# Logits in eight 64x32 tiles, one spread per piece, a ring of five pieces, and token sums at other places of the PE queue

## The reference, cut to what matters

```python
# block 1, per image
y = ln_c(x)                                   # norm over channels, per pixel
g = groupnorm(y, 8 groups) * gn_w + gn_b
x = x + y + w2 @ relu(w1 @ g + b1) + b2
# block 2, per image, tokens = pixels
t = tokens(x); z = ln(t)                      # norm over the 64 channels of a token
logits = z @ gate_w.T + gate_b                # 32 experts
vals, idx = top_k(softmax(logits, over pixels), 8)       # 8 pixels per expert
pooled = sum_k vals[k] * z[idx[k]]            # 64 numbers per expert
out = gelu([pooled, 1] @ weight1) ; out = [out, 1] @ weight2
t[idx[k]] += out * vals[k]                    # the rest of t is unchanged
```

## Time and profile before

| | us |
|---|---|
| median of 3 runs | 639.11 (637.3 to 641.03) |
| the profiled execution | 639.6 |
| its span, first to last instruction | 637.9 |
| PE / DVE / ACT / POOL busy | 535.4 / 487.2 / 435.3 / 189.6 |
| x1 (L948), 64 instructions | 82.1 |
| logits (L409), 1024 matmul records | 69.4 |
| sums (L372) of x, of centred squares, of x1's squares | 74.5 + 35.7 + 34.1 |
| mean granted TensorE clock | 0.935 |

### The profile page before, as it was taken

The page is one execution under the profiler, slowest core; times in us unless marked ns, Lnnn a source line. Parts: engine busy times, 40 slices in busy tenths (PEclk is TensorE's granted clock), DMA queues, the critical chain, the costliest instruction groups (busy, mean ns, idle before and its releaser), DMA issues.

```text
span 637.9 us, 14170 instructions
## 1 busy us (share of the span) xinstructions
PE 535.4 (84%) x5732; PEld 270.3 (42%) x5732; DVE 487.2 (76%) x950; ACT 435.3 (68%) x651; POOL 189.6 (30%) x116
## 2 busy tenths in 40 slices
PE   2749999898998899889989899989887988876982
PEld 1324444444444344444444444444443433434762
DVE  5574556689888988898789878988888687799620
ACT  2463779677976797679767976797677855984110
POOL 1007435023502260217020802080207145121144
PEclk9955999999999999999999999999998998987595
DMA  8960144714471447244634454445401255430000
GB/s 195 195 144 0 68 133 142 188 68 133 133 199 67 134 133 191 76 133 134 168 98 134 115 160 123 133 101 165 133 35 67 76 182 154 146 100 5 6 15 19
DMA packets 26752, 73.38 MB, mean 115 GB/s; under 512 B 4152, under 2 KB 4152, under 8 KB 22592
## 3 DMA queue, kind: packets, MB, share of 16 engines
q1 hardware_dynamic: 25664, 71.44, 40.9%
q0 software_dynamic: 1024, 1.05, 0.6%
HBM read 38.40 MB, written 34.08 MB: 114 GB/s over the span
## 4 chain that ended last, share of the span: by engine, by line
PE 41%; DVE 30%; ACT 13%; issue 12%; DMA 2%; POOL 1%; SPq 0%; ACTq 0%; DVEq 0%; POOLq 0%
PE st L372 11%; ACT junk L801 7%; DVE xs L948 7%; PE cv L383 6%; PE cv L391 6%; PE tl L400 6%; PE bc L494 5%; DVE us L938 5%; DVE lg L936 3%; DVE top_i L1035 2%; ACT tok L766 2%; DVE us L940 2%; DVE cnd L1030 2%; DMA xs<-in_x 2%; PE tl L409 2%
## 5 line engine op out<-in xcount | busy, mean ns | idle before, releaser
L1426 POOL TENSOR_TENSOR xs<-xs,us 128x1024 f32<-128x1024 f32 x64 | 151.2, 2379 | 367.2 <-DVE xs L948 173.4
L948 DVE SCALAR_TENSOR_TENSOR xs<-cv,vecs,xs 128x1024 f32<-128x1024 f32 x64 | 82.1, 1282 | 47.8 <-PE cv L391 47.7
L794 ACT ACTIVATE sqc<-us 128x1024 f32<-128x1024 f32 x64 | 67.5, 1054 | 46.2 <-DVE us L938 45.4
L761 ACT ACTIVATE hid<-cv,b1n 128x1024 f32<-128x1024 f32 x64 | 71.2, 1113 | 36.5 <-PE cv L383 36.0
L938 DVE TENSOR_TENSOR us<-xs,bc 128x1024 f32<-128x1024 f32 x60 | 73.0, 1216 | 19.7 <-PE bc L494 19.3
L400 PEld LDWEIGHTS tl<-ident,xs 128*128 128x128 f32 x512 | 63.8, 195 | 53.9 <-issue 53.9
L372 PE MATMUL st<-xs,stat_w 128*32 128x256 f32 x1024 | 74.5, 413 | 10.5 <-DMA xs<-in_x 9.4
L801 ACT ACTIVATE junk<-us 128x1024 bf16<-128x1024 f32 x64 | 67.3, 1051 | 22.8 <-DVE gsum L940 22.1
L940 DVE CUSTOM_DVE_ANT_0 us<-us,bc 128x1024 f32<-128x1024 f32 x60 | 72.9, 1215 | 11.2 <-PE bc L494 9.9
L400 PE MATMUL tl<-ident,xs 128*128 128x128 f32 x512 | 76.4, 294 | 0.9 <-ACT lg L776 0.9
L409 PE MATMUL tl<-xs,gcen 128*32 128x256 f32 x1024 | 69.4, 389 | 8.0 <-ACT tok L766 7.9
(11 more groups left out here) (210 smaller groups left out, 652.4 us busy)
## 6 DMA issues: line engine op xcount, KB each, us to landing
xs<-in_x SPq DMA_DIRECT2D x64, 512.0 KB, 7.0
out_rows<-tok SPq DMA_DIRECT2D x64, 512.0 KB
us<-in_e_w SPq DMA_DIRECT2D x8, 260.0 KB
xs<-in_e_w SPq DMA_DIRECT2D x8, 256.0 KB
sqc<-out_rows,idx_all POOLq DMA_INDIRECT x16
out_rows<-sqc,idx_all POOLq DMA_INDIRECT x16, 2.1
vecs<-in_b SPq DMA_DIRECT2D x4, 0.2 KB, 14.0
gate_bias<-in_gate_b SPq DMA_DIRECT2D x4, 0.1 KB, 12.3
```

The source lines that it names most:

```text
L948: nc.vector.scalar_tensor_tensor(out=xu, in0=cv[:], scalar=vecs[:, 3:4], in1=xu, op0=ALU.add, op1=ALU.add).then_inc(x1_done, 1)
L1426: nc.gpsimd.tensor_tensor(xu, xu, su, ALU.add).then_inc(s_done, 1)
```

## The change

The logits of a unit become eight matmuls of 64x32 tiles: 64 partitions of one half against that half's 32 columns, half 0 into the first bank of `tl` and half 1 into the second; their copy reads 256 columns of each bank. A piece's columns so hold another order of pixels. An L or E job now works on one whole piece, with four matmuls of 64 partitions by 128 columns from a new constant `spread2`, which 32 small DVE operations build in the prologue; `top_values` of a piece waits for that piece's job alone. `candidates` gets two more operations for the new order. The ring `lg` has five pieces rather than six, and what the tail keeps there moves to `sqx` or closer together.

In the PE queue `x1_square_sums` of group 3 (step 0) move behind conv2 and the spread; `x1_sums` of group 2 (step 6) to the same place, those of group 0 (step 2) behind the logits; `x1_square_sums` of group 1 move from step 5 to step 4, behind the logits (for the last two images, behind the second spread). On ACT the square of unit 3 moves in front of the S square of step 4. The experts' first matmuls wait for the last logits copy rather than the last token copy.

```diff
@@ -33,7 +33,7 @@
 PIECE = HW // 2 // PIECES
-RING = 6
+RING = 5
 CAND = PIECES * K
@@ -49,9 +49,6 @@
 M_JOB, LAST_M_JOB = (7, 0), (7, 1)
-
-L_UNITS = (0, 1, 4, 5)
-
@@ -123,6 +120,7 @@
         spread = sb("spread", [P, 16 * 64], F32R)
+        spread2 = sb("spread2", [P, PIECES * 2 * P], F32R)
         second = sb("second", [P, 1])
@@ -189,16 +187,16 @@
         eq = xs[0][:, HW // 2:HW].rearrange("p (b f i) -> p b f i", b=NB, f=GATHERS)
-        late = lg[:, 2 * PIECE:4 * PIECE]
+        late = lg[:, 2 * PIECE:3 * PIECE]
         pool_f = late[:, 0:NE * NB + 3 * NB]
-        diags = [eq[:, 7 - p % 2].rearrange("p f i -> p (f i)") for p in range(3)] + [late[:, 2 * CH:3 * CH]]
+        diags = [eq[:, 7 - p % 2].rearrange("p f i -> p (f i)") for p in range(3)] + [sqx[:, CH:2 * CH]]
         hg = us[1][:, 0:4 * CH]
...
-        sel = late[:, 3 * CH:3 * CH + 2 * P].rearrange("p (b k e) -> p b k e", b=2, k=4)
+        sel = late[:, CH:CH + 2 * P].rearrange("p (b k e) -> p b k e", b=2, k=4)
         outs8 = us[1][:, 0:CH].rearrange("p (e c) -> p e c", e=8)
@@ -207,6 +205,7 @@
         lgp, pt = tl[:, 0:CH], tl[:, CH:2 * CH]
+        lg_banks = (lgp, pt)
         first_banks = [bc, cv]
@@ -254,7 +253,7 @@
-        RSTD_STEPS, GN_STEPS, LN2_STEPS, TOP_STEPS, MRG_STEPS = 4, 7, 5, 11, 11
+        RSTD_STEPS, GN_STEPS, LN2_STEPS, TOP_STEPS, MRG_STEPS = 4, 7, 5, 13, 11
@@ -264,7 +263,6 @@
-        bc_l = bc[:].rearrange("p (sl i r) -> p i sl r", sl=2, i=2)
@@ -405,9 +403,9 @@
                         for h in range(2):
-                            c, col = 2 * sub + h, UN * u + CH * sl + SUB * sub
-                            mm = pe.matmul(lgp[NE * c:NE * c + NE, SUB * sl:SUB * sl + SUB], gcen[:, NE * h:NE * h + NE],
-                                           xs[par][:, col:col + SUB], start=True, stop=True)
+                            c, col, r = 2 * sl + sub, UN * u + CH * sl + SUB * sub, slice(C * h, C * h + C)
+                            mm = pe.matmul(lg_banks[h][NE * c:NE * c + NE, 0:SUB], gcen[r, NE * h:NE * h + NE],
+                                           xs[par][r, col:col + SUB], start=True, stop=True)
                 mm.then_inc(e_done, 1)
@@ -482,15 +480,18 @@
                     return
+                if kind in ("L", "E"):
+                    for h in range(2):
+                        for w in range(2):
+                            r, col = slice(C * w, C * w + C), P * (2 * k + h)
+                            mm = pe.matmul(bc[:, CH * w + SUB * h:CH * w + SUB * h + SUB], spread2[r, col:col + P], rstd2_s[r, :],
+                                           start=True, stop=True)
+                    mm.then_inc(bc_filled, 1)
+                    return
                 for i in range(2):
                     for sl in range(2):
-                        if kind in ("L", "E"):
-                            u = L_UNITS[k] + 2 * i
-                            c, w = 2 * (u % 2) + sl, 4 * C * (u // 2)
-                            weights, stat = spread[32 * c:32 * c + 32, w:w + 4 * C:2], rstd2_s
-                        else:
-                            c, w = 2 * (k % 2) + sl, 2 * C * (2 * (k // 2) + i)
-                            weights, stat = spread[32 * c:32 * c + 32, w:w + 2 * C], mean_s if kind == "C" else rstd_s
+                        c, w = 2 * (k % 2) + sl, 2 * C * (2 * (k // 2) + i)
+                        weights, stat = spread[32 * c:32 * c + 32, w:w + 2 * C], mean_s if kind == "C" else rstd_s
                         mm = pe.matmul(out[:, CH * sl + SUB * i:CH * sl + SUB * i + SUB], weights,
@@ -523,14 +524,13 @@
                     x1_sums(b, b % 2, NG - 1)
-                    x1_square_sums(b, NG - 1)
                 if s == 1 and p1:
...
                     xc_square_sums(n, 1)
-                if s in (2, 4, 6):
-                    x1_sums(it, par, s // 2 - 1)
-                if s in (3, 5, 7):
+                if s == 4:
+                    x1_sums(it, par, 1)
+                if s in (3, 7):
                     x1_square_sums(it, (s - 3) // 2)
@@ -542,8 +542,16 @@
                     spread_at(it, (s, 1))
+                if s == 0 and b >= 0:
+                    x1_square_sums(b, NG - 1)
+                if s == 6:
+                    x1_sums(it, par, 2)
                 if b >= 0:
                     logits(b, b % 2, u)
+                if s == 2:
+                    x1_sums(it, par, 0)
+                if s == 4 and n + 1 < NB:
+                    x1_square_sums(it, 1)
                 if s == 4:
@@ -555,6 +563,8 @@
                     x_sums(n + 1, s // 2 - 2)
+                if s == 4 and n + 1 >= NB:
+                    x1_square_sums(it, 1)
                 spread_at(it, (s, 2))
@@ -616,7 +626,7 @@
                     pe.wait_ge(ebias_ready, 1)
-                    pe.wait_ge(tok_done, NU * NB)
+                    pe.wait_ge(lcopy_done, NU * NB)
                 for e in range(NE):
@@ -773,7 +783,8 @@
                 col = place(b, u // 2) + CH * (u % 2)
-                nc.scalar.activation(lg[:, col:col + CH], lgp, ACT.Copy).then_inc(lcopy_done, 1)
+                nc.scalar.activation(lg[:, col:col + CH].rearrange("p (h r) -> p h r", h=2),
+                                     tl[:].rearrange("p (h r) -> p h r", h=2)[:, :, 0:SUB], ACT.Copy).then_inc(lcopy_done, 1)
@@ -853,8 +864,10 @@
                     merge_exps(it - 2)
+                if s == 4:
+                    square_x1(b, b % 2, u)
                 square_at(it, (s, 0))
-                if s >= 1:
+                if s >= 1 and s != 4:
                     square_x1(b, b % 2, u)
@@ -927,13 +940,10 @@
                 elif kind in ("L", "E"):
-                    u = L_UNITS[k]
                     if kind == "E":
                         t = NB - 1
-                    dve.wait_ge(lcopy_done, NU * t + u + 3)
-                    lt = lg[:, place(t, u // 2):place(t, u // 2) + 2 * PIECE]
-                    lt = lt.rearrange("p (i w sl r) -> p w i sl r", i=2, w=2, sl=2)[:, u % 2]
-                    ins = nc.vector.tensor_tensor(lt, lt, bc_l, ALU.mult)
+                    dve.wait_ge(lcopy_done, NU * t + 2 * k + 2)
+                    ins = nc.vector.tensor_tensor(piece(t, k), piece(t, k), bc[:], ALU.mult)
                 elif kind == "C":
@@ -1025,8 +1035,7 @@
                 link = Steps(dve, top_steps, TOP_STEPS * t + 2 * i)
-                for k in range(2 * (i // 2), 2 * (i // 2) + 2):
-                    dve.wait_ge(bc_used, scaled(t, k))
+                dve.wait_ge(bc_used, scaled(t, i))
                 link(nc.vector.max(cnd[:, K * i:K * i + K], piece(t, i)))
@@ -1039,9 +1048,12 @@
                 pix = cnd[:, CAND:2 * CAND]
-                link(nc.vector.tensor_scalar(top_hi[:], top_i[:], 0xFFFFFF00, None, ALU.bitwise_and))
+                link(nc.vector.tensor_scalar(top_hi[:], top_i[:], 0xFFFFFE00, None, ALU.bitwise_and))
                 link(nc.vector.scalar_tensor_tensor(out=pix, in0=top_i[:], scalar=rowoff[:], in1=top_hi[:],
                                                     op0=ALU.add, op1=ALU.add))
+                link(nc.vector.tensor_scalar(top_hi[:], top_i[:], SUB, None, ALU.bitwise_and))
+                link(nc.vector.scalar_tensor_tensor(out=pix, in0=top_hi[:], scalar=float(HW // SUB - 1), in1=pix,
+                                                    op0=ALU.mult, op1=ALU.add))
                 link(nc.vector.tensor_tensor(pix, pix, pixbase[:], ALU.add))
@@ -1190,7 +1202,7 @@
                 zz = zs.rearrange("p b g c -> p (b g) c")[:, n0:n1]
-                q = late[:, CH:CH + (n1 - n0) * C].rearrange("p (n c) -> p n c", c=C)
+                q = sqx[:, 0:(n1 - n0) * C].rearrange("p (n c) -> p n c", c=C)
                 mean, var, y, a, rs, ws = (tr[:, i, n0:n1] for i in range(6))
@@ -1229,7 +1241,7 @@
             for r in range(4):
-                nc.vector.memset(rowoff[32 * r:32 * r + 32, :], float(SUB * (r // 2) + HW * (r % 2)))
+                nc.vector.memset(rowoff[32 * r:32 * r + 32, :], float(SUB * r))
             nc.vector.memset(gt[:, 10:11], EPS_C)
@@ -1246,6 +1258,13 @@
             nc.vector.tensor_copy(spread[:].rearrange("p (r y) -> p r y", y=C), tb[:, 0:16].unsqueeze(2).broadcast_to([P, 16, C]))
+            for q in range(4):
+                r = slice(32 * q, 32 * q + 32)
+                for k in range(PIECES):
+                    both = spread2[r, 2 * P * k:2 * P * (k + 1)].rearrange("p (h sl b e) -> p sl h b e", h=2, sl=2, b=2)
+                    picked = tb[r, 4 * k:4 * k + 4].rearrange("p (b h) -> p h b", b=2).unsqueeze(3).broadcast_to([32, 2, 2, NE])
+                    nc.vector.tensor_copy(both[:, q % 2], picked)
+                    nc.vector.tensor_scalar(both[:, 1 - q % 2], picked, 0.0, None, ALU.mult)
...
             nc.vector.tensor_reduce(kmask[:], ident[:].rearrange("p (k e) -> p k e", k=4), AX.X, ALU.add)
```

## The result

The kernel after takes 633.87 us (median of 20 executions, 631.53 to 640.92), the kernel before 638.52 (median of 20, 636.54 to 643.44). The ratio is 0.993, with a 95% interval of 0.9905 to 0.9956: faster by 0.7%. The forecast was 632.0, within 625 to 640. So the time came out as forecast, but several terms of the sum did not, and that of the clock shows how far a right total can be from a right account. A ratio leaves out executions over 1.5% above the fastest of their kernel; of all kernels here only E3 has such, two of its four (658.77 and 660.64).

A forecast was written before the change was run, and what follows sets the result against it. No single engine bounds: PE is late in steps 2 and 0, DVE or ACT mostly elsewhere. Prologue +0.9, image 0 -2.0, images 1-5 -5.25, image 6 -2.9, image 7 -2.0, tail +0.6, clock +3.7: -6.95, to 632 us; range 625 to 640.

The forecast's parts named there:

- The moved sums: Sums moved behind conv2 or the logits on PE: 0.9 us saved in step 2, 0.3 in step 0, per image.
- the new spread: One spread per piece with two row groups instead of four: +0.15 us an image, ahead of conv1 of step 2.
- Steps 5 and 6: conv2 is freed of sums there, but ACT is full: worth 0 in images with exponentials.
- One sign: DVE's wait before x1 of step 2 was to go down from 1.20 to about 0.2 us.
- The logits' shape: Eight 64x32 tiles: logits 0.55 us a unit instead of 1.08, counted as nothing on the path and nothing lost.
- The clock: PE emptied in step 5: granted clock falls in two of images 1 to 7, 1.85 us each, +3.7 (bounds 0 and 13).
- the old fall in image 6: Clock drop in step 4 removed by moved sums: -1.85 us; with the other terms image 6 gains 2.9.
- a granted clock that drops in most images: Named sign that the forecast is wrong, beside images below 63 us.
- The rival with falls in every image: Clock falls in step 5 of every image, 1.85 us each: kernel slower, 643.3 us; chance 0.09.
- Images 0 and 7: Gains of 2.0 us each: image 0 in steps 2, 5 and 6, image 7 from sums moved behind conv2.
- The constants: Thirty-two constants on DVE in the prologue, 0.19 us each: +0.9 us (bounds 0 and +2.8).
- The candidates and the tail: Two more candidates operations of 0.25 us, uncovered in the tail: +0.5, and +0.1 for one spread; +0.6 us.

The follow-up runs named there:

- E3: Kernel after with the old order of sums and squares, keeping new logits, spreads and ring: median 657.67 us, ratio 1.0199 to the kernel before.
- E7: As E4, but with the square sums of group 1 left in step 5 ahead of conv2: 630.8 us, ratio 0.9889.
- E12: As E9, with half of the logits of step 4 issued once more: 628.54 us, ratio 0.9835.
- E4: Kernel before with the new order of sums and squares alone; old logits, spreads and ring: 629.75 us, ratio 0.9865.
- E6: Kernel after with all logits matmuls issued twice: 633.45 us, ratio 0.9929 to the kernel before.
- E1: Kernel after with the square sums of group 1 put back from step 4 to step 5, ahead of conv2: 640.4 us, ratio 1.0018.
- E8: As E3, with all logits matmuls issued twice: 641.68 us, ratio 1.0046.
- E9: As E4, with the square sums of group 1 in two halves, one in step 4, one in step 5: 628.31 us, ratio 0.9838.
- E11: As E7, with half of the logits of step 4 issued once more: 630.5 us, ratio 0.9883.

## Why the prediction was right, and where it was not

**The moved sums.** Right. At full clock the order should give an image -0.9 - 0.3, so 64.0, and 64.15 with the new spread. Measured: step 2 -0.88, step 0 -0.21, and images of 64.1 with the order alone (E7, E12); E4, the order by itself, has more than the whole gain (0.9865). Steps 5 and 6, worth 0 by the forecast: 7.60 + 7.27 = 14.87 in before, 7.27 + 7.58 = 14.85 in E12. Step 5 ends 0.33 sooner and step 6 gives it back, as a full ACT demands. In step 0, x1 comes 0.86 sooner after conv1 than in the earlier trace rows, but the job behind the variance only 0.20, because that now waits for ACT's square of the mean. Rows of after for the steps 0 and 2:

```profile
375.87 1.28 DVE L958 SCALAR_TENSOR_TENSOR xs<-cv,vecs,xs 128x1024 f32<-128x1024 f32 x1 [0.80 <-PE cv L389]
377.72 0.43 DVE L1021 SCALAR_TENSOR_TENSOR st<-st,ta 128x256 f32<-128x256 f32 x1 [0.57 <-ACT ta L822]
...
378.53 1.21 DVE L948 TENSOR_TENSOR us<-xs,bc 128x1024 f32<-128x1024 f32 x1
...
393.13 1.28 DVE L958 SCALAR_TENSOR_TENSOR xs<-cv,vecs,xs 128x1024 f32<-128x1024 f32 x1 [0.73 <-PE cv L389]
```

One sign was read wrongly: the wait before x1 of step 2 was to fall from 1.20 to 0.2, and it is 0.73. DVE's work ahead of it also comes 0.4 sooner in the step, half of it because the wait of 0.27 for the sums behind the logits no longer shows; so the wait shrinks less than the step does.

**The logits' shape, priced at 0 on the path and "nothing lost".** Half right. Almost nothing of it is on the path: in image 1, where E4 keeps the clock, its steps 0 to 5 and those of after agree within 0.02 each; in images 2 to 6 step 1 is 0.07 to 0.09 shorter in after, and E6 adds a second pass at no cost in the whole. The page "TensorEngine Tiling (Array Packing)" of the Trainium skill, section "PSUM Bottleneck", had spoken for a zero; by the steps the trace agrees to within that 0.1. But the shape is not free. In each of three orders the kernel with it is the slower one: 1.0199 against 1 in the old order (E3 and before); 1.0018 against 0.9889 with the square sums of group 1 in step 5 (E1 and E7, which differ in the shape and what it needs alone; intervals apart); 0.993 against 0.9865 in the order of the change (after and E4; the intervals touch). That the emptier waits are the reason is shown in the old order, by E8. In the new order it is not: the profile of E6 has three falls in the main loop where that of after has eight, and its median is the same. And images 2 to 5 of after and of E4 are equally long, with a fall in each; of the 4.6 us between these two spans 1.84 lie in the prologue, 1.90 in images 0 and 1 and 1.49 in the tail, while images 2 to 7 give 0.6 back. The two rows of its price:

```profile
L407 PE MATMUL tl<-xs,gcen 64*32 64x256 f32 x1024 | 42.9, 392 | 7.6 <-ACT tok L776 6.8 <-issue 0.7
...
L487 PE MATMUL bc<-rstd_s,spread 64*128 64x256 f32 x128 | 16.6, 338 | 12.6 <-DVE lg L946 6.6 <-DVE us L948 4.1 <-DVE mrg L941 0.7
```

42.9/64 = 0.67 a unit, not 0.55. The spread by two row groups costs 338 ns a matmul where four row groups took 340: no change, and the +0.15 was not there.

**The clock: the step that failed.** The place was right (PE's queue between conv2 of step 5 and conv1 of step 6), and so was the end of the old fall in image 6: that image gains 2.73, forecast 2.9. Wrong were the count and the price. I took two images of seven at 1.85, the price of the one fall in before; all of images 0 to 6 fall in that step, and image 7 in its step 4 (conv1 of 1.71). The prediction had named a granted clock that drops in most images as a sign of being wrong, and it does. The price of a fall depends on what lies beside it and on how long it lasts. In step 6 ACT is full, 3.83 of the 4.00 us at a clock of 0.57, and hides part of it: images 1 to 5 are 0.7 to 0.8 longer than E12's. The fall of before, 4.01 us at 0.57 (483.29 to 487.30), made image 6 1.85 longer, 0.3 of which image 6 also takes without one (64.46 against 64.13 in E12); with conv1 of step 5 slow an image loses 0.8 in E9 and 1.5 in E11. The 2.97 of E7 belong to a longer fall, 6.53 us at 0.52. So the falls of images 1 to 5 together, 3.8 us, took what I had given to two (3.7), and those of images 0 and 7 are about the part by which these two images fell short of their terms. The rival with falls in every image, 643.3, had the count right and the price wrong; my own number had both wrong, and they nearly cancelled: that this term hardly moved the total was luck.

**Images 0 and 7**, forecast -2.0 each. -0.75 and -1.15. Step 6 of image 0 alone is 1.52 longer (8.37 against 6.85, conv1 at 1.99), and step 4 of image 7 1.04; without these, 2.3 and 2.2. Same cause as above.

**The constants, +0.9.** Nothing. Rows of after, the last constant and DVE's first mean:

```profile
8.76 0.22 DVE L1267 TENSOR_SCALAR spread<-tb 32x128 fp32r<-32x128 f32 x1
...
10.79 0.42 DVE L965 CAST hi<-st 128x256 fp32r<-128x256 f32 x1
```

They run from 4.27 to 8.98, 0.147 each instead of 0.19, and just fill the 4.76 us that DVE waited; the mean starts at 10.79 where it was at 10.78. The row I had, 0.23 for one, was nearly right (0.20 to 0.22 here); I had not taken off enough for the overlap of one with the next, which shows in the distance of their starts. Why the prologue came out 0.35 shorter stays open: conv1 of the first image starts anywhere from 48.96 to 51.84 in the profiled executions of all these kernels.

**The candidates and the tail, +0.6.** 0.79 lost. The two added operations take 0.18 and 0.19 instead of 0.25 each, so they are half of it. The rest stays open: what lies behind the last conv1 takes 82.6 to 84.4 us in the profiled executions of all these kernels.

**What stays open.** Which images fall. Images 3 and 4 of E7 have equal rows and an unequal clock. In after the granted clock drops at 227.00, 291.85, 356.71 and 421.56 us, and the four falls of images 2 to 5 in E4 and in E9 are 64.85 apart in the same way, though other matmuls are hit there. The page "TensorE: Matmul & The Clock Gate" of the Trainium skill, Part 1, says that the window of the activity monitor behind the clock runs freely and does not start anew with a kernel. Both observations agree with this. An image with a fall takes 64.9 in these three kernels, so that the next one meets the same moment again; an image of 64.1 (E7, E12) does not keep that distance. This would explain why some kernels fall in every image, but it is an inference: no run here shifts the same kernel in time to show it.

## What to carry to other kernels

Time saved on an engine that is waiting becomes wait, and on TensorE a longer wait can cost the clock for the work behind it: cut first where TensorE is late, and put movable work into its waits before shortening what fills them. Price a fall of the clock by the place where it would land and by how long it lasts, not by the one fall that the trace happens to show. And when a forecast sums gains and losses, test the terms by undoing them one by one; here the total was right, and one part of the change, kept for its shorter matmuls, was slower than the old logits in each of the three orders in which both were run.

## What was not expected of the hardware

More matmuls made a kernel faster: the same logits issued twice took the ratio from 1.0199 to 1.0046 (E3, E8). And two images of one execution with the same instructions, 3.42 and 3.44 us busy in the same 5.16, came out 2.97 us apart: one kept a granted clock of 1.00 behind that stretch, the other had 0.52 (E7).
